# First cross attention of a four-layer decoder: scores in one pass through keys spread over DRAM, values of four heads side by side

## The reference

```python
B, S, P, D, H = (2, 1024, 256, 256, 16)      # here 16 batches of 112 queries, 375 keys
q = (queries @ wq.T + bq).reshape(b, s, h, dh)                   # dh = 16
k = (patch_representations @ wk.T + bk).reshape(b, p, h, dh)
v = (patch_representations @ wv.T + bv).reshape(b, p, h, dh)
scores = jnp.einsum('bqhd,bkhd->bhqk', q, k) * scale
patch_idx = jnp.cumsum(patch_boundaries, axis=1)
mask = jnp.arange(p)[None, None, :] > patch_idx[:, :, None]
scores = jnp.where(mask[:, None, :, :], jnp.finfo(scores.dtype).min, scores)
attn = jax.nn.softmax(scores, axis=-1)
out = jnp.einsum('bhqk,bkhd->bqhd', attn, v).reshape(b, s, d)
return out @ wo.T + bo
```

## Time and profile before

| | |
|---|---|
| time, median of 3 runs | 4162.86 us (4162.65 to 4162.91) |
| the profiled execution's own time | 4161.14 us |
| its span in the trace | 4159.3 us |
| TensorE busy | 3536.1 us (85%) |
| VectorE busy | 1574.0 us (38%) |
| ScalarE busy | 1536.9 us (37%) |
| GpSimd busy | 1197.4 us (29%) |
| DMA moved | 240.30 MB, mean 58 GB/s |

### The profile page before, as it was taken

The page is one execution under the profiler, slowest core; times in us unless marked ns, Lnnn a source line. Parts: engine busy times, 40 slices in busy tenths (PEclk is TensorE's granted clock), DMA queues, the critical chain, the costliest instruction groups (busy, mean ns, idle before and its releaser), DMA issues. The chain is left out here.

```text
span 4159.3 us, 67079 instructions
## 1 busy us (share of the span) xinstructions
PE 3536.1 (85%) x22014; PEld 2897.3 (70%) x22014; DVE 1574.0 (38%) x3464; ACT 1536.9 (37%) x4297; POOL 1197.4 (29%) x1312
## 2 busy tenths in 40 slices
PE   5999992996897873975999999759599999997999
PEld 4777772885565652654889888658488888885665
DVE  3555552001225541014444544300344444444444
ACT  2333330432224550212555555324255444551111
POOL 0000003002000002014666666410466656661000
PEclk9999995998898976987999999779799999997999
DMA  3000002886110003331000000077200000000001
GB/s 117 12 11 11 11 1 82 304 309 211 51 34 4 0 2 106 116 112 34 9 7 9 9 7 5 3 241 280 74 10 9 9 9 9 8 1 12 23 19 33
DMA packets 102019, 240.30 MB, mean 58 GB/s; under 512 B 24682, under 2 KB 73644, under 8 KB 84012
## 3 DMA queue, kind: packets, MB, share of 16 engines
q1 hardware_dynamic: 94188, 219.82, 16.1%
q0 software_dynamic: 7680, 18.36, 1.7%
HBM read 208.78 MB, written 29.36 MB: 57 GB/s over the span
## 5 line engine op out<-in xcount | busy, mean ns | idle before, releaser
L642 POOL TENSOR_SCALAR L_probs<-L_probs,L_inverse 112x375 f32<-112x375 f32 x512 | 645.2, 1260 | 86.9 <-issue 86.9
L752 DVE TENSOR_REDUCE L_negmax<-bank 112x1 f32<-112x375 f32 x768 | 417.5, 544 | 559.7 <-PE bank L441 344.6
L608 ACT ACTIVATE L_probs<-bank,L_negmax 112x375 f32<-112x375 f32 x768 | 439.4, 572 | 407.1 <-DVE L_negmax L752 407.1
L464 PEld LDWEIGHTS bank<-ident,L_probs 112*125 112x125 f32 x2304 | 360.4, 189 | 108.3 <-ACT L_probs L608 47.1
L640 POOL TENSOR_TENSOR L_inverse<-L_sums,neg_one 112x1 f32<-112x1 f32 x512 | 315.2, 616 | 349.7 <-ACT L_probs L608 344.1
L464 PE MATMUL bank<-ident,L_probs 112*125 112x112 f32 x2304 | 376.0, 271 | 22.0 <-issue 10.3
L596 ACT ACTIVATE L_probsT<-bank 125x336 f32<-125x336 f32 x512 | 231.3, 452 | 315.4 <-PE bank L464 313.3
L479 PE MATMUL bank<-L_probsT,v 125*64 125x112 f32 x3072 | 206.1, 270 | 1.1 <-ACT L_probsT L596 1.1
L453 PE MATMUL bank<-L_kT,L_q 128*112 128x375 f32 x512 | 203.5, 478 | 0.0
L437 PE MATMUL bank<-L_keys_hi,L_q_hh 128*112 128x376 f32 x512 | 184.3, 360 | 8.9 <-DVE L_keys_lo L695 6.5
L581 ACT ACTIVATE v<-bank 125x512 f32<-125x512 f32 x192 | 114.9, 598 | 197.3 <-PE bank L391 197.3
(11 more groups left out here) (272 smaller groups left out, 7070.5 us busy)
## 6 DMA issues: line engine op xcount, KB each, us to landing
L0t_w<-in_F_w SPq DMA_DIRECT2D x70, 1024.0 KB, 5.1
L2t_w<-in_F_w SPq DMA_DIRECT2D x42, 1024.0 KB, 5.2
L_ctxT<-in_ctxT SPq DMA_DIRECT2D x48, 375.0 KB, 3.4
L1t_w<-in_F_w SPq DMA_DIRECT2D x16, 1024.0 KB, 6.2
slots_in<-zeros SPq DMA_DIRECT2D x4, 1792.0 KB, 16.5
L1x_ctxT<-in_ctxT SPq DMA_DIRECT2D x16, 375.0 KB, 3.0
L0t_xs<-slots_in SPq DMA_DIRECT2D x35, 128.0 KB, 6.0
L0t_b<-in_F_b SPq DMA_DIRECT2D x35, 128.0 KB, 6.1
```

The lines of the kernel that those rows point to most:

```text
L464: ins = pe.transpose(psT[h % len(psT)][0:SJ, j * T:(j + 1) * T], probs[h % NB][:, j * SJ:(j + 1) * SJ], core.ident[0:T, 0:T])
L608: act.activation(probs[h % NB][:, :], psS[h % 2][0:T, 0:S], ACT.Exp, bias=negmax[b.par][:, h:h + 1], accum_out=sums[b.par][:, h:h + 1]).th ...
L642: pool.tensor_scalar(probs[h % NB][:, :], probs[h % NB][:, :], inverse[b.par][:, h:h + 1], None, ALU.mult)\
L752: dve.tensor_reduce(negmax[b.par][:, h:h + 1], psS[h % 2][0:T, 0:S], AX, ALU.max, negate=True).then_inc(maxed.sem, 1)
```

## The change

**Scores.** Queries and keys are split into a high and a low part of type fp32r. TensorE multiplies them in a single matmul of 128 rows: two heads share a group of 32 rows, and the four groups of 32 hold high, low, high, low keys, against high, high, low, low queries (the other head's 16 rows are zero). To bring the parts to those rows, SyncE writes them to DRAM and reads them back (`spread`), for each batch: two stores and four loads of keys, then two stores and eight loads of queries, with waits in between. `scores(b, 0)` now waits for all of these loads.

**Values.** The values are kept 32 columns apart for each head (16 of them zero), and are the weights now; `probsT` passes through, 112 columns. Four heads write the four groups of 32 rows of one PSUM bank. ScalarE copies the bank out once a batch (`take_raw`), TensorE turns it back with four transposes (`turn_raw`), and VectorE divides it.

**Order.** `turn` runs two heads behind the scores and the values three to six, with four probability tiles and eight turned ones in place of two; the table `order` is a new one.

```diff
@@ the table, the buffers
-        order = {0: ["K0"], 2: ["K1"], 5: ["O0"], 7: ["Y0", "L0", "L1"], 9: ["Q0"], 10: ["V0"],
-                 12: ["V1"], 14: ["V2"]}
+        order = {0: ["K0"], 1: ["K1"], 3: ["L0", "L1"], 4: ["Q0"], 7: ["O0"], 9: ["Y0"], 11: ["V0"],
+                 13: ["V1"], 15: ["V2"]}
-    lag = 3 if wide else 1
-    NB = 4 if wide else 2
+    lag = 3 if wide else 2
+    NB = 4
+    NT = 4 if wide else 8
+    VH = dh if wide else 32
...
@@ SyncE
+                def spread(b):
+                    sp.wait_ge(taken["K"].sem, taken["K"].at(EC * b.n + EC))
+                    for i, part in enumerate((k_hi, k_lo)):
+                        sp.dma_start(k_dram[i], part[:, :, :].bitcast(F32)).then_inc(k_stored.sem, 16)
+                    sp.wait_ge(k_stored.sem, k_stored.at(32 * b.n + 32))
+                    for quad in range(4):
+                        sp.dma_start(keys4[b.par][32 * quad:32 * quad + 32, :, :].bitcast(F32),
+                                     core.spread_k[quad % 2].rearrange("c (g r) s -> r (c g) s", r=32))\
+                            .then_inc(keys_here.sem, 16)
+
+                    sp.wait_ge(q_split.sem, q_split.at(b.n + 1))
+                    for i, part in enumerate((q_hi, q_lo)):
+                        sp.dma_start(q_dram[i], part[:, :, :].bitcast(F32)).then_inc(q_stored.sem, 16)
+                    sp.wait_ge(q_stored.sem, q_stored.at(32 * b.n + 32))
+                    for quad in range(4):
+                        for e in range(2):
+                            rows = slice(32 * quad + 16 * e, 32 * quad + 16 * e + 16)
+                            sp.dma_start(q4[b.par][rows, e::2, :].bitcast(F32),
+                                         core.spread_q[quad // 2].rearrange("c (g e r) t -> e r (c g) t", e=2, r=16)[e])\
+                                .then_inc(q_here.sem, 16)
...
                 with sp.Fori(0, (B - 2) // 2) as i:
-                    for k in (2, 3):
-                        b = Batch(i, k)
-
-                        sp.wait_ge(made["V"].sem, made["V"].at(count("V%d" % (NV - 1), b + -2)))
-                        load(b)
+                    spread(Batch(i, 0))
+                    next_load(Batch(i, 2))
+                    spread(Batch(i, 1))
+                    next_load(Batch(i, 3))
+                spread(Batch(0, B - 2))
+                spread(Batch(0, B - 1))
@@ TensorE
-                        pe.wait_ge(taken["Q"].sem, taken["Q"].at(NQ * b.n + NQ))
-                        pe.wait_ge(taken["K"].sem, taken["K"].at(EC * b.n + EC))
+                        pe.wait_ge(q_here.sem, q_here.at(128 * b.n + 128))
+                        pe.wait_ge(keys_here.sem, keys_here.at(64 * b.n + 64))
 
                         pe.wait_ge(barred_ready.sem, barred_ready.at(b.n + 1))
 
-                    pe.matmul(psS[h % 2][0:T, 0:S], core.ident_b[0:T, 0:T], barred[b.par][:, :],
+                    pe.wait_ge(exped.sem, exped.at(H * b.n + h - 1))
+                    pe.matmul(psS[h % 2][0:T, 0:SP], core.ident_b[0:T, 0:T], barred[b.par][:, :],
                               start=True, stop=False)
-                    pe.matmul(psS[h % 2][0:T, 0:S], q[b.par][:, h, :], kT[b.par][:, h * dh // P, :],
+                    pe.matmul(psS[h % 2][0:T, 0:SP], q4[b.par][:, h, :], keys4[b.par][:, h // 2, :],
                               start=False, stop=True).then_inc(scored.sem, 1)
...
+                def quad_values(b, h):
+
+                    pe.wait_ge(probsT_ready.sem, probsT_ready.at(H * b.n + h + 4))
...
+                    at = h // 4 * T
                     for j in range(J):
-                        ins = pe.matmul(bank[0:T, h % G * dh:(h % G + 1) * dh], probsT[h % 2][:, j, :],
-                                        v[b.par][0:SJ, j, h * dh:(h + 1) * dh], start=(j == 0), stop=(j == J - 1))
+                        for i in range(4):
+                            ins = pe.matmul(psO[0][i * VH:(i + 1) * VH, at:at + T],
+                                            v[b.par][0:SJ, j, (h + i) * VH:(h + i + 1) * VH], probsT[(h + i) % NT][:, j, :],
+                                            start=(j == 0), stop=(j == J - 1))
                     ins.then_inc(pv_done.sem, 1)
+
+                def turn_raw(b):
+
+                    pe.wait_ge(raw_ready.sem, raw_ready.at(b.n + 1))
+
+                    pe.wait_ge(o_ready.sem, o_ready.at(b.n))
+                    for g in range(H // 4):
+                        ins = pe.transpose(core.bank[5][0:T, g * P:(g + 1) * P], raw[:, g * T:(g + 1) * T], core.ident[:, :])
+                    ins.then_inc(o_turned.sem, 1)
...
-                        if not wide and not (b_first and h < 2):
-                            values(*before(b, h, 2))
+                        if not wide and h % 4 == 2 and not (b_first and h < 6):
+                            quad_values(*before(b, h, 6))
+                        if not wide and h == 5 and not b_first:
+                            turn_raw(b + -1)
@@ ScalarE
+                        act.activation(k_hi[:, m, 0:S], bank[:, 0:S], ACT.Identity, bias=bk[:, m:m + 1])\
+                            .then_inc(k_high.sem, 1)
...
+                def take_raw(b):
+
+                    act.wait_ge(pv_done.sem, pv_done.at(H // 4 * b.n + H // 4))
+                    act.activation(raw[:, :], psO[0][:, 0:H // 4 * T], ACT.Copy).then_inc(raw_ready.sem, 1)
@@ VectorE
+                    if p[0] == "K" and not wide:
+                        dve.wait_ge(k_high.sem, k_high.at(EC * b.n + m + 1))
+                        dve.scalar_tensor_tensor(out=k_lo[:, m, 0:S], in0=bank[:, 0:S], scalar=bk[:, m:m + 1],
+                                                 in1=k_hi[:, m, 0:S].bitcast(F32), op0=ALU.add, op1=ALU.subtract)\
+                            .then_inc(taken["K"].sem, 1)
...
+                            ins = dve.tensor_scalar(qs[:, c, :], bank[:, c * T:(c + 1) * T], bq[:, c:c + 1], scale,
+                                                    ALU.add, ALU.mult)
+                        ins.then_inc(taken["Q"].sem, 1)
+                        dve.drain()
+                        dve.tensor_copy(q_hi[:, :, :], qs[:, :, :])
+                        dve.drain()
+                        dve.tensor_tensor(q_lo[:, :, :], qs[:, :, :], q_hi[:, :, :].bitcast(F32), ALU.subtract)\
+                            .then_inc(q_split.sem, 1)
...
+                    for part in q4:
+                        dve.memset(part[:, :, :].bitcast(F32), 0.0)
```

More of the change, by code:

```diff
@@ L196, in cross_attention @@
         probs = [sb(f"probs{i}", [T, S]) for i in range(NB)]
-        probsT = [sb(f"probsT{i}", [SJ, J, T]) for i in range(NB)]
+        probsT = [sb(f"probsT{i}", [SJ, J, T]) for i in range(NT)]
         negmax = [sb(f"negmax{i}", [T, H]) for i in range(2)]
@@ L214, in cross_attention @@
             last_key = sb("last_key", [T, B])
-            keys = sb("keys", [T, S])
-            headmask = sb("headmask", [P, P // dh])
-            barred = [sb(f"barred{i}", [T, S], BF16) for i in range(2)]
+            keys = sb("keys", [T, SP])
+            barred = [sb(f"barred{i}", [T, SP], BF16) for i in range(2)]
             barred_ready = core.counter("barred_ready")
@@ L345, in _, with next_load @@
                     return
+                k_dram = [core.spread_k[i].rearrange("c p s -> p c s") for i in range(2)]
+                q_dram = [core.spread_q[i].rearrange("c p t -> p c t") for i in range(2)]
+                def spread(b):
[17 more added lines that the diff above has]
+                                .then_inc(q_here.sem, 16)
+                def next_load(b):
+                    sp.wait_ge(made["V"].sem, made["V"].at(count("V%d" % (NV - 1), b + -2)))
+                    load(b)
                 load(Batch(0, 0))
@@ L528, in tail @@
                     else:
+                        turn(b, H - 2)
                         turn(b, H - 1)
-                        values(b, H - 2)
-                        values(b, H - 1)
+                        quad_values(b, H - 4)
+                        turn_raw(b)
                     where = last_slots()
@@ L560, in _ @@
                 act.wait_ge(weights.sem, weights.at(16 * nweights))
+                if not wide:
+                    act.wait_ge(v_zeroed.sem, v_zeroed.at(1))
                 def take(p, b, at):
@@ L603, in heads @@
                     for h in range(H):
+                        if not wide and h == 3 and not b_first:
+                            take_raw(b + -1)
                         if wide and not (b_first and h < lag):
@@ L658, in _ @@
                     return
+                for part in v:
+                    ins = pool.memset(part[:, :, :], 0.0)
+                ins.then_inc(v_zeroed.sem, 1)
+                pool.drain()
                 rstd(Batch(0, 0))
@@ L832, in tail @@
                     if not wide:
-                        take_probsT(b, H - 1)
+                        for h in range(H - lag, H):
```

(17 more changed lines are left out.)

87 lines of the change are left out of this document (47 added, 40 removed).

## The result

The changed kernel takes 3992.13 us in the median of four runs (3987.03 to 3997.67); the kernel before took 4162.75 in runs beside it. The ratio is 0.9594, with a 95% interval of 0.9577 to 0.9611. The forecast was 4033 with a range from 3998 to 4092: the kernel became faster, as forecast, and by 6 us more than the range holds. These four runs lie up to 10.6 us apart, so single differences of a few microseconds are not read as effects.

The account below looks back on a forecast made before the run. TensorE bounded layer 0's attention; afterwards the DMA chain would. Start +23.9, batch 0 25.9 for 32.1, 14 periods of 25.9 for 35.84, last batch 18 for 28.3, +1.5: -130 from 4161.1, so 4031, median 4033 us (3998 to 4092).

Parts of the forecast that it names:

- The other layers keep their order.: Outside layer 0's attention stage, some 14% of the program: the other layers keep their order; no time term.
- first scores: Start of layer 0's attention: first scores at 75.0 us in place of 52.6, +22.4.
- batch 0, with its slow clock: Layer 0's first batch: 25.9 in place of 32.1 us, plus 1.5 for TensorE leaving idle at the lower clock.
- 14 periods: Layer 0's steady batches: 14 periods of 25.9 us each in place of 35.84.
- last batch to the end: Layer 0's last batch: 18 us in place of 28.3, its end 1.5 longer for one more copy and turn.
- chain: Layer 0's key and query stores and loads through DRAM: 20.2 us after `taken` at 5.7, setting the period of 25.9.
- rival 1: Layer 0: the DMA chain is hidden and the engines' 24.9 us decide; 4014, down to 3998 us; chance 0.15.
- quad: Layer 0's values of four heads, run side by side: 0.95 us in place of 2.11.
- rival 3: Layer 0's values do not run four at once: 4045 us two at a time, near 4110 singly; chance 0.07.
- I allow 1.0: Layer 0's loop through two score banks: 1.0 us a batch of waiting, making the engines' 23.9 into 24.9.
- rival 2: Layer 0: TensorE's clock falls after idling before each batch; about 29.4 us a batch, 4085 us; chance 0.17.
- Rivals 4 and 5: Layer 0's DMA chain longer: 22.5 to 27.8 us, 4070 to 4155 (0.07); or from 28.4, slower than before (0.04).

Follow-up runs that it names:

- after_pad32: The changed kernel with 64 satisfied waits (32 TensorE instructions) ahead of layer 3's attention, putting its loop where the kernel before has it; 4015.46 us.
- four padded kernels: The changed kernel with 64, 128, 192 or 576 satisfied waits ahead of layer 3's attention, layer 0 the same; 4015.46, 3988.31, 3989.23 and 4027.58 us.
- keys_twice: The changed kernel with the four key loads issued twice, first into a spare tile that nobody reads; 4122.43 us.
- scores_only: The changed kernel with values computed as before (16 columns a head, three matmuls a head), keeping spread and one-pass scores; 4073.85 us.

## Why the prediction was wrong

The range was missed through one step, and the mechanism of another was wrong while its sum held.

**"The other layers keep their order."** This is the step that failed. They do keep their order, and I took it to mean that they keep their time: the sum has no term for them. They gave 39 us: 34.5 in layer 3's stretch, by the place of the code, and 4.4 ahead of it, which is within what that stretch varies. In the unchanged part of the profile the term could have been seen: 108 instruction packets over the run (63 in the kernel after), and issue pauses of 2.4 us in layer 3. That the change moves TensorE's stream by 32 instructions, and so could end such a stall or begin one, belonged among the rivals with 30 to 40 us to either side. Without it the forecast holds: with both kernels at the slow place the ratio is 0.9673 (after_pad32, 0.9639 to 0.9708), and 4162.75 times that is 4027 (4012 to 4041); with both at a fast place it is 3989.23 / 4122.26 = 0.9677. The change itself is worth some 3.2 to 3.3% (2.9 to 3.6 by the interval of the first), and 4027 lies 6 us under the forecast.

**Layer 0, term by term**, from the profiled execution, and from those of the four padded kernels:

| term | forecast | measured | four padded kernels |
|---|---|---|---|
| first scores (from 52.6) | 75.0, +22.4 | 73.97, +21.4 | 74.2 to 75.6 |
| batch 0, with its slow clock (from 32.1) | 27.4 | 27.4 | 28.7 to 29.4 |
| 14 periods (from 501.8) | 362.6 | 357.6 | 357.5 to 358.8 |
| last batch to the end (from 36.9) | -8.8 | -8.0 | -8.1 to -7.3 |
| sum | -130 | -135.5 | -133.5 to -131.0 |

That batch 0 came out at the 27.4 of the forecast is luck: in the other executions it is 1.3 to 2.0 longer, by the longer wait ahead of the second batch. In them the sum is within 1 to 3.5 us of the forecast, since this and the shorter periods work against each other.

**The period.** The forecast had 25.9, set by a chain of 5.7 + 20.2 against engines of 24.9. It is 25.4, set by the engines, and the chain of 5.6 + 19.1 = 24.7 lies hidden beneath it by 0.7. So rival 1 (0.15) was the true one in its mechanism, but with engines at 25.4 and not at 24.9. Both limits were right within 5%; which of two limits one microsecond apart decides could not be read from them, and it made 5 us.

- Values: a quad was put at 0.95 with 0.83 as its lowest end, and owns 0.82 by the same measure. Four at once was right (rival 3 falls); entering and leaving the narrow tiles costs 0.82 less the 6 x 0.093 of the passes = 0.26, where the pair of layer 2 gave 0.27. The allowance for eight instructions in each step was not needed. The Trainium skill (TensorEngine Tiling, Key Properties) says that a change of tiling mode drains TensorE. The trace agrees with such a price of 0.26, and the 0.6 to 0.7 that the prediction gave to a quad without it did not come.
- A head without values 0.65 against 0.67, `turn_raw` 0.44 against 0.45, `taken` 5.6 against 5.7: right.
- "I allow 1.0" for the loop through two banks held for what it priced: the waits for `exped` are 0.35 a batch (4.6 in 13) and those for `probsT` 0.63 (8.2 in 13), together 1.0, and not the over 2 us that the prediction named as the sign against it. What it had no term for is the other 1.1, the waits for `normed` and `hT`: work that VectorE and ScalarE deliver a little after TensorE, now faster, comes to it. The earlier trace rows have 0.5 of idle time in a batch before.
- TensorE's own work of 23.9 was 23.3, mostly the quads (4 x 0.13). With 2.1 of pauses for the 1.0 allowed it made 25.4.

**The chain.** Stores 3.6 against 4.4 (285.17 to 288.76); key loads with the query stores behind them 10.0 against 8.6 + 1.5; query loads 5.4 against 5.3 (298.77 to 304.2). The loads to 32 rows, of which no row stood in the trace, ran as I took them from x's rate. keys_twice prices them better: 1.54 MB more took 7.3 us, 211 GB/s. The Trainium skill (SBUF — State Buffer, Door 1: The DMA port swizzle) has 32 partitions reach half of the ports, which of its 435 GB/s would be an estimated 218. The 211 agrees, but the four loads together fill all 128 rows, and that the ports are their limit was not tried.

**The clock** (rival 2, 0.17): granted 1.00 in all steady batches, in which no wait was over 0.8 us. It fell to 0.50 while TensorE idled for the first queries (60 to 70 us) and was 0.66 in 70 to 80, which is what the forecast's 1.5 us for batch 0 stand for. Rivals 4 and 5 fall with the chain of 19.1. VectorE's two clears at the start took 1.55 each, 3.1, where I had 3.5.

## What to carry to other kernels

When an edit changes the number of an engine's instructions, look in the unchanged loops behind it for "issue" pauses and for packets of the instruction queue: a loop of 1580 TensorE instructions cost 31 to 38 us more or less in the traces (26 to 29 in the medians) by its place alone, and satisfied waits ahead of it are a cheap way to try another place. Compare versions at like places, or the gain of an edit is mixed with that of its shift. Compare a stage over several executions, too: one profile of the changed kernel had the end of layer 0 2.0 to 4.6 us ahead of four others whose code is the same there. Where two limits come out within a microsecond, count on the larger and keep both mechanisms; and when TensorE's work shrinks by a third, its short waits for the other engines grow (here from about 0.5 to 2.1 us a batch), so that two savings of 5.8 and 6.7 give 10.4 together.

## What the runs showed of the hardware

- The place of a large loop in TensorE's stream decides whether its code is brought again at each turn: 45 packets of 16.4 KB in 500 us against 2, 9 a turn against none, with pauses of up to 2.6 us, at places 256 instructions apart; 32 instructions to either side of one such place it is gone. In one run (scores_only, layer 2) a loop did so in two turns and not in the later ones.
- Values of four heads in four groups of 32 columns do run at once: 24 fp32 records of 112 columns own 0.82 us, of which 0.26 is entering and leaving.
- TensorE's clock can be granted 0.50, its lower level of 1.2 GHz, for 37.5 us while it is fully busy (scores_only, 177.5 to 215 us; in the 10 us from 160 to 170 it was 97% busy with 1.00 granted, and in 170 to 177 it paused twice, for 0.4 and 0.5 us). No other run here showed this in the steady stage without long pauses of TensorE, and its cause stays open.
